# Box layer: the gathers start after the last convolution, and the boxes are made in three pieces

## The reference

```python
integ = jnp.cumsum(jnp.cumsum(x, axis=-1), axis=-2)          # integral image
h1 = gelu(conv3x3(x, w1_off) + b1_off)
sub = conv1x1(h1, w2_off) + b2_off                            # four offsets a pixel
...                                                           # box edges from the offsets, at least 2 pixels
area = jnp.clip((h_max - h_min) * (w_max - w_min) * tp_w * tp_h / 4, 1.0, H * W)
scale = conv1x1(gelu(conv3x3(x, w1_mod) + b1_mod), w2_mod) + b2_mod
A, Bt, Ct, D = (grid_sample(integ, corner) for corner in corners)   # bilinear, four pixels each
return (A + D - Bt - Ct) / (area * scale)
```

## Time and profile before

| | us |
|---|---|
| median of 3 runs | 7519.23 |
| lowest, highest | 7515.94, 7521.47 |
| profiled execution, its own time | 7518.81 |
| its span in the trace | 7517.1 |
| box layer, first gather | 6699.06 |
| box layer, last gather starts | 7507.19 |

### The profile page before, as it was taken

One profiled execution on the slowest core, in us unless ns is written; L12 is line 12 of the kernel. 1 busy time (PEld: TensorE's weight loads), 2 busy tenths in 40 slices (PEclk: granted clock), 3 DMA queues, 4 the chain that ended last, 5 costly groups with the idle time before them and its releaser, 6 DMA issues. The chain is left out here.

```text
span 7517.1 us, 169527 instructions
## 1 busy us (share of the span) xinstructions
PE 6082.4 (81%) x69188; PEld 2639.6 (35%) x69188; DVE 6727.2 (89%) x6038; ACT 5237.8 (70%) x5319; POOL 3441.3 (46%) x1801
## 2 busy tenths in 40 slices
PE   6899999999999999897688888888888888765100
PEld 3433333333333333564233333333333333343000
DVE  8899999999999999797799999999999999863666
ACT  3488888888888888333588888888888888620000
POOL 2000000000000000000499999999999999744666
PEclk9999999999999999998899999999999999976555
DMA  3200000000000000000200000000000000121222
GB/s 66 56 12 10 9 9 11 10 10 9 9 12 9 10 9 6 8 6 11 71 6 6 6 6 6 6 6 6 6 6 6 6 6 6 32 82 47 66 74 76
DMA packets 146946, 153.67 MB, mean 20 GB/s; under 512 B 66540, under 2 KB 125708, under 8 KB 144924
## 3 DMA queue, kind: packets, MB, share of 16 engines
q1 hardware_dynamic: 120224, 89.43, 4.6%
q0 software_dynamic: 24576, 50.36, 2.6%
q10 hardware_dynamic: 1440, 3.75, 0.3%
HBM read 101.83 MB, written 37.95 MB: 19 GB/s over the span
## 5 line engine op out<-in xcount | busy, mean ns | idle before, releaser
L1891 POOL TENSOR_TENSOR k_image<-k_image,s_b 128x1024 f32<-128x1024 f32 x1152 | 2702.6, 2357 | 117.1 <-ACT k_image L1804 83.4
L797 ACT ACTIVATE att_prob<-att_scores,a_bound,a_temp 128x1024 f32<-128x1024 f32 x2048 | 2356.7, 1202 | 361.8 <-PE att_scores L747 361.8
L808 DVE TENSOR_TENSOR att_prob_lo<-att_prob 128x1024 f16<-128x1024 f32 x2048 | 2440.1, 1238 | 169.2 <-ACT att_prob L797 158.8
L732 POOL TENSOR_TENSOR k_image<-k_image,att_rden 48x512 f32 x32 | 68.6, 2143 | 2893.5 <-DVE att_rden L829 2893.5
L1804 ACT COPY k_image<-h_du 128x1024 f32<-128x1024 f32 x1152 | 1166.4, 1013 | 322.8 <-PE h_du L1738 322.4
L1854 DVE TENSOR_TENSOR_SCAN h_state_odd<-h_keep,k_image 128x1024 f32<-128x1024 f32 x576 | 1321.9, 2332 | 0.3 <-ACT h_keep L1810 0.3
L1810 ACT ACTIVATE h_keep<-h_keep,h_decay 128x1024 f32<-128x1024 f32 x1152 | 1256.7, 1091 | 75.2 <-PE h_keep L1727 51.4
L747 PE MATMUL att_scores<-att_queries,att_keys 32*128 32x512 f16 (+1 forms) x20480 | 1292.9, 377 | 19.7 <-DMA att_keys<-qk_halves 17.0
L764 PE MATMUL att_sums<-att_prob,a_values 128*64 128x512 bf16 x8192 | 1129.2, 396 | 0.0
L1727 PE MATMUL h_keep<-h_rows,h_spread 128*128 128x512 bf16 x2304 | 699.5, 385 | 511.0 <-DVE h_state_odd L1854 263.2
L1738 PE MATMUL h_du<-h_rows,h_spread 128*128 128x512 bf16 x2304 | 701.2, 386 | 35.8 <-DMA h_rows<-parts 33.5
(11 more groups left out here) (309 smaller groups left out, 6454.0 us busy)
## 6 DMA issues: line engine op xcount, KB each, us to landing
y_rows<-h_y_sb SPq DMA_DIRECT2D x1024, 3.0 KB
att_queries<-qk_halves SPq DMA_DIRECT2D x124, 128.0 KB, 2.2
parts<-t_part SPq DMA_DIRECT2D x48, 192.0 KB, 2.5
h_rows<-parts SPq DMA_DIRECT2D x128, 72.0 KB
b_shared<-cells,b_index POOLq DMA_INDIRECT x512
qk_halves<-qkv_hi SPq DMA_DIRECT2D x128, 48.0 KB, 1.6
cells<-b_shared SPq DMA_DIRECT2D x4, 1536.0 KB, 5.1
att_keys<-qk_halves SPq DMA_DIRECT2D x32, 128.0 KB, 2.9
```

Of the source, the lines that this page charges most:

```text
L797: nc.scalar.activation(prob[:, u % RING, :], scores[:, u % SLOTS_S, :], ACT.Exp, bias=bound[:, 0:1], scale=temp[:, 0:1]).then_inc(prob_rea ...
L808: nc.vector.tensor_tensor(prob_lo[:, u % RING, :], prob[:, u % RING, :], prob_hi[:, u % RING, :], ALU.subtract).then_inc(low_ready, 1)
L1891: nc.gpsimd.tensor_tensor(drive[k % 3], du_sb[k % 3], b[:, c * CH:(c + 1) * CH], ALU.mult).then_inc(drive_ready, 1)
```

## The change

GpSimd no longer waits piece by piece: before its first gather it waits for all 32 convolution groups (`convolved`) and for all boxes (`boxed`). The boxes are made in three pieces of 48, 48 and 32 rows (`BOX_ROWS`), the index part, the weights and the scale part being separate functions. DVE makes them all before its first row, except the scale part of rows 80 to 127 (`scales` of 16-row pieces 5, 6 and 7), which stands behind groups 6, 10 and 14. The subtractions `split_low` come before the boxes. The addition of the bias is split: the four offsets in `indices`, the 48 scales in `scales`. Additions to the image start at group 5. `heads` keeps its size of 128 rows; the tile `stats` is no longer allocated by the layer but passed in; two pairs of small tiles share their place.

```diff
-ADDS_FROM = 6
+ADDS_FROM = 5
+BOX_ROWS = ((0, 3 * PIECE_Y), (3 * PIECE_Y, 6 * PIECE_Y), (6 * PIECE_Y, H))
...
             for k in range(2):
                 pool.wait_ge(table_stored[k], 16 * NCHUNK // 2)
+            pool.wait_ge(convolved, NGROUP)
+            pool.wait_ge(boxed, len(BOX_ROWS))
             for y in range(H):
-                if y % PIECE_Y == 0:
-                    pool.wait_ge(boxed, y // PIECE_Y + 1)
                 wait_past(pool, weighed, y + 1 - GOT)
...
-            def piece(p):
-                dve.wait_ge(heads_copied, (p + 1) * PIECE_Y // GROUP_Y)
-                box.piece(p, head_rows(p * PIECE_Y, PIECE_Y), b2, boxed)
+            def indices(k):
+                y0, y1 = BOX_ROWS[k]
+                dve.wait_ge(heads_copied, y1 // GROUP_Y)
+                box.indices(y0, y1)
...
-            piece(0)
             for k in range(1, 4):
                 split_low(k)
+            for k, (y0, y1) in enumerate(BOX_ROWS):
+                indices(k)
+                box.weights(y0, y1)
+                for p in range(y0 // PIECE_Y, y1 // PIECE_Y):
+                    if p <= 4:
+                        box.scales(p)
...
-                p, first = divmod(i, PIECE_Y // GROUP_Y)
-                if first == 0 and p + 1 < NPIECE:
-                    piece(p + 1)
+                p, turn = divmod(i, PIECE_Y // GROUP_Y)
+                if turn == 2 and p + 4 < NPIECE and p:
+                    box.scales(p + 4)
...
+    def scales(self, p):
+
+        rows = slice(p * PIECE_Y, (p + 1) * PIECE_Y)
+        tt = self.nc.vector.tensor_tensor
+        scales = self.heads[:, rows, 4:HEADS]
+        self.then(tt(scales, scales, self.b2[:, 4:HEADS].unsqueeze(1).broadcast_to([P, PIECE_Y, C]), ALU.add))
+        self.then(tt(scales, scales, self.area[:, rows].unsqueeze(2).broadcast_to([P, PIECE_Y, C]), ALU.mult))
+        self.then(self.nc.vector.reciprocal(scales, scales))
```

More of the change, by code:

```diff
@@ L2335, in row @@
                 dve.wait_ge(reduced, y + 1)
-                nc.vector.tensor_tensor(mean[:, y, :], total[:, :], head_rows(y, 1)[:, 0, 4:HEADS],
+                nc.vector.tensor_tensor(mean[:, y, :], total[:, :], heads[:, y, 4:HEADS],
                                         ALU.mult).then_inc(divided, 1)
@@ L2401, in then @@
         self.dve.wait_ge(self.step, self.count)
[L2403 to L2408, removed]
-        tt, ts, stt = nc.vector.tensor_tensor, nc.vector.tensor_scalar, nc.vector.scalar_tensor_tensor
[L2410 to L2416, removed]
-        for e in range(2):
[L2418 to L2425, removed]
@@ new lines, in indices @@
+    def indices(self, y0, y1):
+        nc, then, r = self.nc, self.then, y1 - y0
+        mean, dev, edge, pos, whole, cell, above = (self.mean[:, 0:r], self.dev[:, :, 0:r], self.edge[:, 0:r],
+                                                    self.pos[:, 0:r], self.whole[:, 0:r], self.cell[:, 0:r], self.above[:, 0:r])
+        rows = slice(y0, y1)
+        tt, ts, stt = nc.vector.tensor_tensor, nc.vector.tensor_scalar, nc.vector.scalar_tensor_tensor
+        flat = lambda t: t.rearrange("p y a e -> p (y a e)")
+        offsets = self.heads[:, rows, 0:4]
+        off = offsets.rearrange("p y (a e) -> p y a e", e=2)
+        then(tt(offsets, offsets, self.b2[:, 0:4].unsqueeze(1).broadcast_to([P, r, 4]), ALU.add))
+        then(tt(mean, off[:, :, :, 0], off[:, :, :, 1], ALU.add))
+        then(ts(mean, mean, 0.5, None, ALU.mult))
+        for e in range(2):
+            then(tt(dev[:, e], off[:, :, :, e], mean, ALU.subtract))
+        then(stt(out=edge[:, :, :, 0], in0=dev[:, 0], scalar=-MIN_OFFSET, in1=dev[:, 1], op0=ALU.min, op1=ALU.min))
+        then(stt(out=edge[:, :, :, 1], in0=dev[:, 0], scalar=MIN_OFFSET, in1=dev[:, 1], op0=ALU.max, op1=ALU.max))
+        then(tt(pos.rearrange("p y a e -> p (y a) e"), edge.rearrange("p y a e -> p (y a) e"),
+                self.centre[:, rows, :].rearrange("p y a -> p (y a)").unsqueeze(2).broadcast_to([P, 2 * r, 2]), ALU.add))
@@ L2438, in piece, with weights @@
                          in1=cell[:, :, 1, ey], op0=ALU.mult, op1=ALU.add))
-        self.dve.sem_inc(boxed, 1)
-        fraction = above
+        self.dve.sem_inc(self.boxed, 1)
+    def weights(self, y0, y1):
+        nc, then, r = self.nc, self.then, y1 - y0
+        edge, pos, cell, fraction, part, size = (self.edge[:, 0:r], self.pos[:, 0:r], self.cell[:, 0:r], self.above[:, 0:r],
+                                                 self.part[:, 0:r], self.size[:, 0:r])
+        rows = slice(y0, y1)
+        area = self.area[:, rows]
+        tt, ts, stt = nc.vector.tensor_tensor, nc.vector.tensor_scalar, nc.vector.scalar_tensor_tensor
+        flat = lambda t: t.rearrange("p y a e -> p (y a e)")
         then(tt(flat(fraction), flat(pos), flat(cell), ALU.subtract))
[L2443 to L2446, removed]
+        then(ts(part[:, :, :, 0, 0], fraction[:, :, :, 0], -1.0, None, ALU.add))
+        then(ts(part[:, :, :, 0, 1], fraction[:, :, :, 0], -1.0, None, ALU.mult))
+        then(ts(part[:, :, :, 1, 0], fraction[:, :, :, 1], -1.0, 1.0, ALU.mult, ALU.add))
+        then(nc.vector.tensor_copy(part[:, :, :, 1, 1], fraction[:, :, :, 1]))
         for ey in range(2):
@@ L2451, in piece @@
                     then(tt(dst[:, :, ex, dy, :], part[:, :, 0, ex, :],
[L2452 to L2458, removed]
+                            part[:, :, 1, ey, dy:dy + 1].broadcast_to([P, r, 2]), ALU.mult))
+        then(tt(size, edge[:, :, :, 1], edge[:, :, :, 0], ALU.subtract))
+        then(stt(out=area, in0=size[:, :, 1], scalar=AREA, in1=size[:, :, 0], op0=ALU.mult, op1=ALU.mult))
+        then(ts(area, area, 1.0, float(NPIX), ALU.max, ALU.min))
+    def scales(self, p):
[5 more added lines that the diff above has]
+        self.then(self.nc.vector.reciprocal(scales, scales))
 def real_fourier(m=PATCH):
@@ L2600, in program @@
         rows = scan_layer(nc, image, gmean, norm, sems, ident, d, stats, kept_image, kept)
-        box_layer(nc, image, gmean, norm, sems, ident, d, out, *rows)
+        box_layer(nc, image, gmean, norm, sems, ident, d, stats, out, *rows)
 def kernel(**inputs):
```

32 lines of the change are left out of this document (14 added, 18 removed).

## The result

The changed kernel took 7556.5 us (median of 5 runs, 7553.8 to 7558.1) where the kernel before took 7521.5 (5 runs): 1.0046 of it, 95% interval 1.0035 to 1.0057. It is slower, by 35 us. The forecast was 7497 us with a range up to 7510, so both the time and the side were wrong.

A forecast was written before the change was run, and what follows sets the result against it. The kernel was taken to end a fixed tail after the last gather, gathers being delayed by 167.1 us of waits and stretching; all goes, less 140.2 for the later start and 5 remaining: 21.9 us saved, 7497 us, range 7489 to 7510.

The forecast's parts named there:

- Start of the first gather: GpSimd, after all convolutions and the index part: first gather at 6839.3 us, 140.2 us later than before.
- Convolutions, boxes, weights and scales hidden; no stall for products: Work before and beside the gathers: covered, at no cost; all 12 waits for products, 147.3 us, go.
- The remainder s: Longer gathers while DVE catches up after a scale step: between 0 and 14 us, taken as 5.
- the upper bound of 14: Limit on s: three scale steps, each some 13 rows long at 0.04 to 0.09 us a gather, 14 us.
- at that pace 511 intervals take 641.0 us: Row of 512 gathers: undisturbed, one every 1.254 us, read from the last 46 gathers.
- the 0.7 us grid: Once gathers have run some 40 us, every other engine issues only on a grid of about 0.7 us.
- the 0.4 us that the forecast added for the median: Step from span to time: the profiled execution took 0.4 us less than the median of the runs.
- The fixed tail: After the last gather's start: span ends 9.9 us later, and the execution takes 1.7 us more than its span.
- the second: Rival: products meet gathers in every group of rows, pace 1.345 us, price 46 us, time 7538; 5 in 100.
- The first rival: DVE trails the gathers all through and products meet them: price 26.4 us, time 7518, no change; 12 in 100.
- The convolutions were not slower: Rival: convolutions before the first gather take 5.9 us a group, price 28 us, time 7525; 4 in 100.
- The rule on the port: Two-input VectorE instruction and SBUF-reading GpSimd instruction contend, the second blocks; at most 122 us, time near 7610.

The follow-up runs named there:

- h4: The changed kernel, unaltered, run again on chip 7, of the kind without slow pace; 7497.4 us, 1.0169 of the kernel before.
- g1: Changed kernel with all additions, all stores and most transposes behind the last row, on chip 1, which has the slow pace; 7576.7 us.
- f2: The changed kernel, unaltered, run again on chip 14, which has the slow pace; 7558.9 us, 1.0034 of the kernel before.
- g2: Changed kernel with each row's product computed from one full-size input, weighting left out, on chip 1, which has the slow pace; 7560.1 us.
- g4: Changed kernel with GpSimd waiting for each piece of boxes but not for the convolutions, on chip 1, slow pace; 7538.9 us, 1.0008 of the kernel before.
- j1: Changed kernel with two short stops of GpSimd, before rows 44 and 86, on chip 6, slow pace; 7556.1 us, 1.0043 of the kernel before.
- g3: Changed kernel with two GpSimd pauses of 25 us, before rows 40 and 80, on chip 1, which has the slow pace; 7563.1 us.
- h3: Changed kernel with each gather bringing half its elements, on chip 7, without slow pace; 7522.6 us, 1.0199 of the kernel before.
- e4: Changed kernel with GpSimd waiting for each piece of boxes but not for the convolutions, on chip 15, without slow pace; 7460.6 us.

## Why the prediction was wrong

*Start of the first gather*: right, 6840.9 for 6839.3, and 6842.0 in h4. *Convolutions, boxes, weights and scales hidden; no stall for products*: right, one wait of 0.5 us in place of 147.3.

*The remainder s*, "I take 5": this is the term that failed. From first to last gather the sum has 646.0 us (641.0 + 5); it took 689.0. s is 48, not 5, and the upper bound of 14 was far too low. The premise under it, that "at that pace 511 intervals take 641.0 us", was read from the last 46 gathers; they belong to a row of 80 gathers that follow a wait of 11.8 us and run for 101 us. The longest run in the trace of before without a stop of over 2 us is 112 gathers long, and the pace falls after some 190. The trace of before could not show the slow pace itself, and I took a pace of 46 for a pace of 512. It did show the 0.7 us grid, which the forecast took for a trouble of the other engines alone; g1's gathers stand on it too. The sum's errors add up: start 1.6, pace 43.0, end of the span 15.8 - 9.9 = 5.9, outside the span 10.8 - 1.7 = 9.1; 59.6, less the 0.4 us that the forecast added for the median; 7556.5 - 7497.3 is 59.2.

*The fixed tail*: also wrong, by 15 us of those. The changed kernel, f2, g2, g4 and j1 end in the slow pace and take 10.0 to 11.0 us beyond their span; the kernel before 1.7, and on chip 14 3.1, g1, whose end has no gathers, 1.8, and all runs on chips without slow pace 1.8 to 2.3. g3, with slow gathers only at the very end, has 9.7. Of the 5.9 us more inside the span none lies in the program's own last steps: the last addition starts 6.4 us after the last gather in the changed kernel (7536.31 - 7529.89) and in h4 alike. What is worked off there was not seen.

*The rivals*: the second, with 5 in 100, named a slower kernel and nearly the size (1.345 us a gather; measured 689.0/511 = 1.348). That is luck, since its mechanism is wrong: DVE is not behind (it waits 283.2 us), and most long gathers of g1 meet no product. The first rival needs a trailing DVE as well. The convolutions were not slower. The rule on the port was no guide here: by it products before gathers cost time, which h3 shows, but the order was already the good one, as h4 shows with 5 gathers over 1.2 us.

*Where the forecast holds*: on a chip without the slow pace its time comes out, 7497.4 in h4 for 7497: the start is 2.7 us late, s is 2.9 instead of 5, the rest of the difference is in the end. But there the kernel before takes 7371 to 7373, because the waits that the change was to remove do not exist. The change loses on both kinds: the later start costs some 140 us, and it removes waits of 144 us where the chip then limits the gathers, or none where it does not.

## What to carry to other kernels

A pace read from a short stretch is no pace for an unbroken run: look for the longest unbroken run in the trace, and if the change makes a longer one, give the range that gap. When many engines wait at once for nothing that the profile names, ask whether the limit is shared, and whether the engine that your sum rests on could meet it too. Run the kernel before on a second chip before building a change on those waits. No version here beats the kernel before: e4's, which starts early, is equal on a chip with the limit and 1.2% slower without.

## What the runs showed of the hardware

The six chips fall into two kinds. On 14, 1 and 6 the kernel before took 7531.2, 7531.4 and 7522.9 us, near the 7521.5 of the comparison above; on 15, 7 and 10 it took 7370.9, 7372.9 and 7370.6. Each chip was used in one sitting only, so that the kind belongs to the chip and not to the moment is the nearest reading and not shown. The difference lies in the box layer: the first gather starts at 6699.06 and at 6704.60 on chip 10, the last at 7507.19 and 7363.20. In the first kind unbroken gathers run at 1.25 us for about 190 of them and at 1.40 after that; with many matmuls beside them the other engines come to the 0.7 us grid after 40 us. The slow gathers stand on a grid of the same step, one every two steps. The slow pace behaves like a store of some 28 us that fills at 0.15 us a gather and empties while no gather is issued; the common step of 0.70 us makes it likely that grid and slow pace are one limit. That other engines' instructions fill the store faster is argued and not shown, and g1, where fewer instructions bought nothing, speaks against a plain count of them.

What is stored stays open. It is not the data of the gathers: in the changed kernel it lands within 3.2 us throughout. The Trainium skill ("NOTIFIC — the notification-queue block", section "7.1 Overflow: three behaviours, one of which stalls the engine") says that the block which writes trace records always holds back its producers inside rather than lose a record there, and marks this as partly inferred. Such a limit would be shared by all engines; no run here shows that it is at work. Every execution on record comes with a span and a granted clock from such records, so no run tells whether the slow pace is there without them. Whether the limit goes by bytes or by gathers wasn't settled either, since the only run with half the bytes fell on a chip without it.
